# q moved between x's two first tiles, and biases loaded as columns, in a fused gating and ternary feed-forward kernel

## The reference, cut to what matters

```python
# x (128, 32, 256), cond (128, 128); _L0_cond_ref(x, cond, W3, b3, W2, b2):
q_emb = relu(cond @ W3 + b3)                          # (128, 256)
c = (32 * x + sum(x, axis=1, keepdims)) * q_emb[:, None, :]
c = relu(c @ W2 + b2)                                 # (128, 32, 256)
# _L0_ffn_ref(c, w1, w3, w2), each weight made ternary: s = mean|w|, round(w/s) clipped to -1..1, times s
g = silu(c @ w1q.T) * (c @ w3q.T)                     # hidden size 682
out = x + g @ w2q.T
```

## Time and profile before

| what | us |
|---|---|
| median of 3 runs | 166.07 (165.84 to 166.11) |
| profiled execution, device time | 166.31 |
| profiled execution, span of the instructions | 164.5 |
| TensorE busy | 160.6 (98%) |
| VectorE busy | 116.1 (71%) |
| ScalarE busy | 88.9 (54%) |

### The profile page before, as it was taken

The page is one execution under the profiler, slowest core; times in us unless marked ns, Lnnn a source line. Parts: engine busy times, 40 slices in busy tenths (PEclk is TensorE's granted clock), DMA queues, the critical chain, the costliest instruction groups (busy, mean ns, idle before and its releaser), DMA issues.

```text
span 164.5 us, 2291 instructions
## 1 busy us (share of the span) xinstructions
PE 160.6 (98%) x765; PEld 132.5 (81%) x765; DVE 116.1 (71%) x186; ACT 88.9 (54%) x163; POOL 55.2 (34%) x52
## 2 busy tenths in 40 slices
PE   7999999999999999999999999999999999999992
PEld 3988777888887888788887888788887888788892
DVE  2166999988978891888548891888647880666863
ACT  3148788525744566355744566255744567255540
POOL 5014033321361266204841266203841267001600
PEclk9999999999999999999999999999999999999999
DMA  5998656666566597000160006000160006100063
GB/s 155 298 357 158 103 81 96 97 98 100 90 98 96 91 234 130 11 4 0 23 104 0 0 4 112 17 0 0 22 108 4 2 0 108 19 0 4 15 112 128
DMA packets 67412, 12.67 MB, mean 77 GB/s; under 512 B 63216, under 2 KB 67144, under 8 KB 67400
## 3 DMA queue, kind: packets, MB, share of 16 engines
q1 hardware_dynamic: 67104, 12.33, 38.1%
q10 hardware_dynamic: 296, 0.20, 0.5%
HBM read 8.32 MB, written 4.19 MB: 76 GB/s over the span
## 4 chain that ended last, share of the span: by engine, by line
PE 98%; DVE 0%; issue 0%
PE bank L516 49%; PE bank L559 21%; PE bank L444 17%; PE bank L543 3%; PE bank L429 3%; PE bank L478 1%; PE bank L459 1%; PE bank L491 1%; PE bank L471 0%; PE bank L453 0%; DVE xo L746 0%; PE bank L481 0%; PE bank L483 0%; PE bank L487 0%; DVE blank L688 0%
## 5 line engine op out<-in xcount | busy, mean ns | idle before, releaser
L516 PE MATMUL bank<-c_hi,T 128*128 128x512 f32 (+1 forms) x176 | 69.2, 393 | 0.0
L516 PE MATMUL bank<-c_lo,T 128*128 128x512 f32 (+1 forms) x176 | 68.8, 391 | 0.0
L380 ACT ACTIVATE silu<-bank,checked 128x512 f32<-128x512 f32 (+1 forms) x48 | 33.1, 689 | 51.5 <-PE bank L516 51.3
L731 DVE SCALAR_TENSOR_TENSOR gf<-bank,out_scale,silu 128x512 f32<-128x512 f32 (+1 forms) x42 | 31.3, 744 | 34.4 <-PE bank L516 30.8
L516 PEld LDWEIGHTS bank<-c_hi,T 128*128 128x128 f32 (+1 forms) x176 | 32.7, 186 | 7.6 <-issue 0.2
L516 PEld LDWEIGHTS bank<-c_lo,T 128*128 128x128 f32 (+1 forms) x176 | 32.8, 186 | 7.3
L268 POOL TENSOR_TENSOR x<-y,qT 128x512 f32<-128x512 f32 x12 | 13.7, 1144 | 53.3 <-DVE y L649 53.3
L444 PE MATMUL bank<-x,W_sb 128*128 128x256 f32 x128 | 29.3, 380 | 0.0
L559 PE MATMUL bank<-g_hi,T 128*128 128x512 f32 x70 | 28.5, 407 | 0.0
L739 DVE TENSOR_TENSOR g_lo<-gf,g_hi 128x512 fp32r<-128x512 f32 x40 | 28.4, 711 | 0.0
L387 ACT CAST g_hi<-gf 128x512 fp32r<-128x512 f32 x40 | 24.5, 612 | 5.4 <-DVE gf L731 5.1
(11 more groups left out here) (71 smaller groups left out, 113.9 us busy)
## 6 DMA issues: line engine op xcount, KB each, us to landing
xb<-in_x_dram SPq DMA_DIRECT2D x64, 64.0 KB, 2.5
out_dram<-turned SPq DMA_DIRECT2D x28, 128.0 KB, 2.7
xo<-in_x_dram SPq DMA_DIRECT2D x3, 256.0 KB, 4.3
w_sb<-in_L_ffn_w_dram SPq DMA_DIRECT2D x2, 384.0 KB, 5.9
w_sb<-in_L_ffn_w_dram SPq DMA_DIRECT2D x1, 682.0 KB, 7.7
w_sb<-in_L_ffn_w_dram SPq DMA_DIRECT2D x2, 256.0 KB
xo<-in_x_dram SPq DMA_DIRECT2D x1, 512.0 KB, 3.9
xo<-in_x_dram SPq DMA_DIRECT2D x2, 128.0 KB, 2.6
```

What stands on the lines that cost most here:

```text
L380: nc.scalar.activation(silu[r, m % 2, :], h1[j % 2][r], ACT.Silu, scale=checked[r, 0:1]).then_inc(silu_done, 1)
L516: last = pe.matmul(dst[j % 2][0:w, :], T13[:, k, col:col + w], part[:, g % NC, k, :], start=(i == 0), stop=(i == len(passes) - 1))
L731: nc.vector.scalar_tensor_tensor(out=gf[r, m % 3, :], in0=second, scalar=out_scale[r], in1=silu[r, m % 2, :], op0=ALU.mult, op1=ALU.mult). ...
```

## The change

It does four things. (1) The biases are loaded straight into `b_cols`, one float32 to a partition, by two DMAs from ScalarE's queue; the rows, TensorE's transpose of them and VectorE's copy are gone, and ScalarE waits for `got_b` itself before it makes `qT`. (2) The matmuls for q stand in `project_q()`, called in `mix_x(0)` between x's first and second tile. (3) `project_c(0)` comes ahead of `mix_x(2)`, and in SyncE's queue W2 ahead of half 2. (4) Six matmuls of 128 columns on zeros (`keep_busy`) are added: four ahead of `mix_x(1)`, two behind it.

```diff
--- before.py
+++ after.py
@@ -67,7 +67,6 @@
             return ctx.enter_context(nc.semaphore(name))
 
         cond_sb = sb("cond_sb", [P, Q], F32)
-        b_rows = sb("b_rows", [2 * DC, P], F32)
         condT = sb("condT", [P, B], F32)
         b_cols = sb("b_cols", [P, 2 * DC], F32)
         b3_col = [b_cols[:, c:c + 1] for c in range(DC)]
@@ -128,7 +127,6 @@
         o_turned = [bank[:, 4 + c, :] for c in range(DC)]
         o_last = bank[:, 6, 0:D]
         condT_ps = bank[:, 4, 0:B]
-        b_cols_ps = bank[:, 3, 0:2 * DC]
         qT_ps = bank[:, 5, 0:DC * B].rearrange("p (c b) -> p c b", c=DC)
         sums_ps = [bank[:, b, 0:2] for b in (4, 5, 7)]
 
@@ -158,7 +156,6 @@
         zeroed = sem("zeroed")
         blank_ready, mix_ready = sem("blank_ready"), sem("mix_ready")
         condT_done, condT_copied = sem("condT_done"), sem("condT_copied")
-        b_cols_done, b_cols_copied = sem("b_cols_done"), sem("b_cols_copied")
         q_done, q_ready = sem("q_done"), sem("q_ready")
         abs_done, sums_done, limit_done = sem("abs_done"), sem("sums_done"), sem("limit_done")
         scale_step = sem("scale_step")
@@ -218,8 +215,8 @@
             for t in range(HTT):
                 sp.dma_start(kept(0)[:, t], x_v[0, :, t]).then_inc(got_first[t], 16)
             load_half(1)
+            sp.dma_start(W2_sb[:], W2.rearrange("(c p) n -> p c n", p=P)).then_inc(got_W2, 16)
             load_half(2)
-            sp.dma_start(W2_sb[:], W2.rearrange("(c p) n -> p c n", p=P)).then_inc(got_W2, 16)
 
             sp.wait_ge(zeroed, 2)
             load_w13(w1_sb, w1, got_w1)
@@ -300,14 +297,15 @@
         def _(act):
             act.dma_start(cond_sb[:], cond).then_inc(got_cond, 16)
             act.dma_start(W3_sb[:], W3).then_inc(got_W3, 16)
-            act.dma_start(b_rows[0:DC, :], b3.rearrange("(c p) -> c p", p=P)).then_inc(got_b, 16)
-            act.dma_start(b_rows[DC:2 * DC, :], b2.rearrange("(c p) -> c p", p=P)).then_inc(got_b, 16)
+
+            act.dma_start(b_cols[:, 0:DC], b3.rearrange("(c p) -> p c", p=P), allow_slow_non_contiguous=True).then_inc(got_b, 16)
+            act.dma_start(b_cols[:, DC:2 * DC], b2.rearrange("(c p) -> p c", p=P), allow_slow_non_contiguous=True).then_inc(got_b, 16)
 
             act.wait_ge(const_ready, 2)
             nc.scalar.activation(warm[:], ident[:, 0:1], ACT.Silu)
             act.wait_ge(condT_done, 1)
             nc.scalar.copy(condT[:], condT_ps).then_inc(condT_copied, 1)
-            act.wait_ge(b_cols_copied, 1)
+            act.wait_ge(got_b, 16 * 2)
             act.wait_ge(q_done, DC)
             for c in range(DC):
                 nc.scalar.activation(qT[:, :, c, :], qT_ps[:, c, :].rearrange("p (h b) -> p h b", b=HB), ACT.Relu,
@@ -417,11 +415,10 @@
                 if n == 3:
 
                     pe.wait_ge(x1_done, 2)
-                if n == 2:
-
-                    pe.wait_ge(b_cols_done, 1)
                 mixed = mixed_of(n)
                 for t in range(HTT):
+                    if n == 0 and t == 1:
+                        project_q()
                     if n == 0:
                         pe.wait_ge(got_first[t], 16)
                     for c in range(DC):
@@ -430,6 +427,13 @@
                                          kept(n // HALVES)[:, n % HALVES * HTT + t, c * P:(c + 1) * P], mix[:],
                                          start=True, stop=True)
                 last.then_inc(mixed_done, 1)
+
+            def project_q():
+                pe.wait_ge(got_W3, 16)
+                pe.wait_ge(condT_copied, 1)
+                for c in range(DC):
+                    pe.matmul(qT_ps[:, c, :], W3_sb[:, c * P:(c + 1) * P], condT[:], start=True, stop=True
+                              ).then_inc(q_done, 1)
 
             def project_c(n):
                 pe.wait_ge(x1_done, n + 1)
@@ -479,21 +483,19 @@
             pe.wait_ge(const_ready, 2)
             pe.wait_ge(got_cond, 16)
             pe.transpose(condT_ps, cond_sb[:], ident[:]).then_inc(condT_done, 1)
-            for _ in range(2):
-                pe.matmul(bank[:, 7, 0:P], blank[:], blank[:], start=True, stop=True)
+            def keep_busy(n):
+                for _ in range(n):
+                    pe.matmul(bank[:, 7, 0:P], blank[:], blank[:], start=True, stop=True)
+
+            keep_busy(2)
             pe.wait_ge(mix_ready, 6)
             mix_x(0)
-            pe.wait_ge(got_b, 16 * 2)
-            pe.transpose(b_cols_ps, b_rows[:], ident[0:2 * DC, 0:2 * DC]).then_inc(b_cols_done, 1)
-            pe.wait_ge(got_W3, 16)
-            pe.wait_ge(condT_copied, 1)
-            for c in range(DC):
-                pe.matmul(qT_ps[:, c, :], W3_sb[:, c * P:(c + 1) * P], condT[:], start=True, stop=True
-                          ).then_inc(q_done, 1)
+            keep_busy(4)
             mix_x(1)
-            mix_x(2)
+            keep_busy(2)
             pe.wait_ge(got_W2, 16)
             project_c(0)
+            mix_x(2)
             project_c(1)
             mix_x(3)
             pe.wait_ge(const_ready, 4)
@@ -694,8 +696,6 @@
             dve.wait_ge(mix_ready, 5)
             nc.vector.scalar_tensor_tensor(out=mix[:], in0=ident[:], scalar=float(S), in1=mix[:], op0=ALU.mult,
                                            op1=ALU.add).then_inc(mix_ready, 1)
-            dve.wait_ge(b_cols_done, 1)
-            nc.vector.tensor_copy(b_cols[:], b_cols_ps).then_inc(b_cols_copied, 1)
             dve.wait_ge(q_ready, DC)
             parts = [slice(part[0] * D, (part[-1] + 1) * D) for part in PARTS]
             scale_mixed(0)
```

## The result

The changed kernel takes 167.34 us (median of 6, 167.18 to 167.66); the kernel before took 166.24 in the runs beside it (6, 165.84 to 166.69). The ratio is 1.0075, with a 95% interval of 1.0056 to 1.0095: slower by 1.1 us by the medians, by about 1.25 us by the ratio. The forecast was 166.2 us, no change that can be told, with a range of 165.75 to 167.0, so it was wrong. In a later sitting the same kernel lay at 167.91 against 166.19, ratio 1.0093 (1.0072 to 1.0114). The ratios are of fast executions alone, which leaves out one of that sitting's six, at 171.22 us.

What follows compares the result with a forecast made beforehand. TensorE was taken as the bound; 0.07 us for its stream plus 0.07 for the gap ahead of q, other terms 0, made about +0.15, from 166.07 to 166.2 us, with an 8-in-10 range of 165.75 to 167.0.

Steps and rivals of the forecast that it cites:

- What bounds the kernel: Whole kernel: TensorE is the bound, busy 160.6 of 164.5 us; only work or waits taken from its stream gain.
- Stream after without waits: TensorE's start: 0.45 us freed at the low clock goes into six zero matmuls, leaving TensorE 0.07 us behind.
- the gap: TensorE ahead of q, waiting for condT: 0 to 0.2 us, central 0.15, costing 0.07, at most 0.35.
- Bias landing: Bias loads ahead of qT, x1(0) and project_c(0): landing at 5.85 us against about 6.4, so hidden.
- rival 1: TensorE's wait for x1(0) ahead of project_c(0): biases land late, 167.0 us for landing at 7.2, 168.5 at 8.7; chance 0.15.
- Other traffic, taken as 0: Loads of half 1, W2, half 2, w1 and w3 beside the 512 bias pieces: no cost to TensorE, 0 us.
- The clock rises at 6.89 as before: TensorE around half 1: the rate goes from 1.2 to 2.4 GHz at 6.89 us, as in the kernel before.
- rival 3: TensorE's start: added work hides, no gap at q, clock rises a little earlier; 0.3 to 0.5 us faster, 165.7; chance 0.16.
- Rival 2: TensorE from half 1's mixing: clock rises later, 167.1 us, or 168.8 with project_c(0) also at the low rate; chance 0.06.

Runs made afterwards that it cites:

- e1: Changed kernel without its two bias loads, b_cols set to zero by VectorE; 166.23 us, ratio 1.0007 to the kernel before.
- e9: Kernel before with each bias load as 8 pieces of 128 bytes, turned by VectorE, no bias transpose on TensorE; 166.94 us, ratio 1.0034.
- e11: Changed kernel with biases in 8-piece blocks turned by VectorE, no zero matmuls, old order of half 2, project_c(0) and W2's load; 167.52 us, ratio 1.0078.
- e13: The changed kernel once more, nothing altered, in a later sitting; 167.91 us, ratio 1.0093 to the kernel before.
- e2: Changed kernel with the bias columns loaded into a tile nobody reads, so their traffic stays but not the wait; 166.80 us, ratio 1.0044.
- e4: Kernel before with the biases loaded as columns alone: old order, no zero matmuls, no bias transpose; 167.09 us, ratio 1.0079.
- e10: Changed kernel with each bias load as 8 pieces of 128 bytes, turned into columns by VectorE; 168.09 us, ratio 1.0106 to the kernel before.
- e14: e10 with its two bias loads issued behind ScalarE's copy of condT; 172.54 us, ratio 1.0367 to the kernel before.
- e6: Changed kernel with each bias load reading two neighbouring elements to a partition, 128 pieces of 8 bytes; 166.51 us, ratio 1.0026.

## Why the prediction was wrong, point by point

- *What bounds the kernel*: right, TensorE, and the loss lies in its first 13 us, most of it in waits.
- *Stream after without waits*, +0.07 with the gap another 0.07: about right in total. e1 has +0.12 (interval -0.17 to +0.40), though not by the parts I added up: in its profile the rate rises sooner, and in its chain the projection begins at 7.54 and not at 7.87. The gap ahead of q was small: q at 4.48, `condT` copied at 4.05 + 0.25 in ScalarE's timeline, as worked out (4.30).
- *Bias landing*: the step that failed. I took 5.85 us, W3's time of 2.9 plus 0.82 for 512 pieces, against a limit of 6.4. They landed at 6.90 and 7.49 in the two profiles. Neither term fitted. W3 was issued a microsecond sooner; even the eight-piece loads of e9 to e11 needed 3.7 to 4.5 us from their later issue. And 0.82 is the time that SyncE takes to issue an `xb` load, not what the pieces cost the DMA engines; and these, which I took as full, ran at a share of 0.67 beside the pieces. The mechanism is rival 1's, place and all, to which I gave 0.15; for landings at 6.90 and 7.49 its price gives 166.7 and 167.3, both about 0.6 under the medians of their sittings (167.34 and 167.91).
- *Other traffic, taken as 0*: failed too. W2 was to land "by 2.25 + 4.9 = 7.15 at the latest", 7.9 with the whole load; it took 5.8 us and landed at about 8.05, and 6.1 us in e13. Half 1 was to be "no more exposed than before except to that load": it took 4.0 us in the first profile, as before, but 5.1 in e13's. e2 puts the traffic at about 0.6 us, half of the loss; the rest, e2 to the changed kernel, some 0.5 to 0.8, is the wait for the biases.
- *The clock rises at 6.89 as before*: I read one execution as if it were the rule. In others it rose two to three microseconds sooner (e13, e2, e4). Then TensorE asks for half 1 up to a microsecond sooner (in e13 at about 5.9 us and not at 6.7), and the cover I counted for it isn't there. What the early rise gains is spent before the projection: e13 asks for x1(0) at about 8.05, no sooner than the first profile's 7.81. An early rise, my rival 3, gives nothing back here: the loads take it.
- *Rival 2* (late clock) didn't happen in either profile of this kernel; e10 and e11 show that it is real. e14's low clock is another matter, it followed a long wait.

The split between traffic and wait comes from kernels of different sittings and from intervals some 0.3 us wide either way, so its halves are rough. How much of the late landing is due to the pieces and how much to the time of issue is open, and so is why the engines move less while the pieces pass.

## What to carry to other kernels

A load of single elements on the start's crowded DMA engines is not a 2 KB load: count its pieces, and ask both when it lands and what it pushes back. Moving a chain earlier gains nothing where its next input lands late, as q's biases did here; find that input's landing before paying for the move. And if the clock may rise at different times, work the slack out for the early rise too, since it takes cover away from loads.

## What was not expected of the hardware

- 512 pieces of 4 bytes took 4.77 and 5.36 us from the second issue to landing in the two chains of the changed kernel, and cost 0.6 us by slowing other loads (e2), while the DMA engines' share fell to 0.67 (4 to 6 us); 256 pieces of 8 bytes cost 0.8 us less in all (e6).
- Issuing a load into four partitions, 8 pieces of 128 bytes, took 1.11 us and the next 0.55, though it is 1 KB; 256 single elements took 0.46 and 0.49.
- The same program had the high rate from about 5 us on in one execution (e13) and from 6.8 in another, with no difference in what TensorE did ahead of it.
- One wait of 5.3 us brought the lower clock for the following six (e14, in an execution of 174.12 us): the median is 172.54 us, against 168.09 for e10.
